# Second attention's query scaling taken to VectorE in a PSUM bank, and its trailing parts from GpSimd to VectorE

## The reference

```
x = x + tanh(g_xattn) * cross_attention(layernorm(x), ctx)          # stage one
y = layernorm(x)                                                     # stage two
q, k, v = y @ Wq.T + bq, y @ Wk.T + bk, y @ Wv.T + bv                # 16 heads of 32
q = (q / norm(q, per head) + query_embedding) * softplus(temperature)
h = softmax(q @ k.T / sqrt(32)) @ v
x = x + tanh(g_ffn) * ((h * gates(h)) @ Wp.T + bp)
```

## Time and profile before

| | |
|---|---|
| median of 3 runs | 5229.36 us |
| the profiled execution's own time | 5233.06 us |
| its span, first to last instruction | 5231.3 us |
| TensorE (PE) matmuls busy | 4810.8 us, 92% |
| VectorE (DVE) busy | 3102.1 us, 59% |
| ScalarE (ACT) busy | 2599.0 us, 50% |
| GpSimd (POOL) busy | 3365.1 us, 64% |
| mean granted TensorE clock | 0.964 |

### The profile page before, as it was taken

The page is one execution under the profiler, slowest core; times in us unless marked ns, Lnnn a source line. Parts: engine busy times, 40 slices in busy tenths (PEclk is TensorE's granted clock), DMA queues, the critical chain, the costliest instruction groups (busy, mean ns, idle before and its releaser), DMA issues.

```text
span 5231.3 us, 67135 instructions
## 1 busy us (share of the span) xinstructions
PE 4810.8 (92%) x21696; PEld 2752.7 (53%) x21696; DVE 3102.1 (59%) x3776; ACT 2599.0 (50%) x4673; POOL 3365.1 (64%) x2667
## 2 busy tenths in 40 slices
PE   4999999999999999998998998998998998989998
PEld 3564555555555555564554554554654544645644
DVE  4555555454546464566766757657657666667663
ACT  2444444343434343546646546546456456456364
POOL 1656656564746565637857757667578487478587
PEclk8999999999999999999999999999999999999998
DMA  7353434343343434332233231322222322322320
GB/s 231 93 143 102 121 108 123 111 119 115 93 129 85 137 85 129 90 100 72 53 97 73 55 108 49 81 81 66 75 79 73 89 60 63 89 75 55 97 49 25
DMA packets 285207, 481.08 MB, mean 92 GB/s; under 512 B 32832, under 2 KB 165440, under 8 KB 275648
## 3 DMA queue, kind: packets, MB, share of 16 engines
q1 hardware_dynamic: 284864, 476.79, 33.6%
HBM read 223.14 MB, written 50.33 MB: 52 GB/s over the span
## 4 chain that ended last, share of the span: by engine, by line
PE 48%; DVE 7%; issue 3%; ACT 2%; POOL 1%; SPq 0%; DMA 0%; ACTq 0%; DVEq 0%; POOLq 0%
PE aux L834 14%; PE acc L937 10%; PE aux L897 9%; PE scores L920 9%; DVE nm L1275 4%; PE aux L949 2%; PE aux L958 1%; DVE rs L1225 1%; PE aux L878 1%; POOL added_f L812 1%; PE aux L854 1%; ACT probs L1122 1%; SPq L729 0%; DMA stack<-ck_lo 0%; ACT xs L1030 0%
## 5 line engine op out<-in xcount | busy, mean ns | idle before, releaser
L1275 DVE TENSOR_REDUCE nm<-aux 128x1 f32<-128x1024 f32 x1536 | 1844.1, 1221 | 1208.8 <-PE aux L897 1205.5
L812 POOL TENSOR_TENSOR added<-added,probs 128x512 f32<-128x512 f32 x1433 | 1805.8, 1297 | 966.2 <-PE acc L937 690.8
L1122 ACT ACTIVATE probs<-scores 128x512 f32<-128x512 f32 x2151 | 1190.0, 597 | 915.4 <-PE scores L920 881.2
L920 PE MATMUL scores<-stack 128*128 128x512 f32 x4096 | 1353.0, 420 | 102.2 <-ACT probs L1122 58.8
L897 PE MATMUL aux<-stack 96*128 96x512 f32 (+1 forms) x3072 | 1023.8, 422 | 132.5 <-DVE nm L1275 96.5
L920 PEld LDWEIGHTS scores<-stack 128*128 128x128 f32 x4096 | 740.7, 191 | 716.7 <-issue 276.4
L937 PE MATMUL acc<-probs,vh 128*32 128x512 f32 (+1 forms) x4302 | 979.8, 623 | 62.2 <-ACT vh L1089 37.9
L897 PEld LDWEIGHTS aux<-stack 96*128 96x128 f32 (+1 forms) x3072 | 529.4, 191 | 618.7 <-DVE nm L1275 319.5
L812 POOL TENSOR_TENSOR added_f<-added_f,probs 128x512 f32<-128x512 f32 x537 | 676.8, 1294 | 57.9 <-PE acc L937 35.9
L834 PE MATMUL aux<-xT_hi,wqk 128*128 128x512 f32 x1536 | 580.6, 407 | 14.8 <-ACT qwork L1061 6.9
L1122 ACT ACTIVATE more<-scores 128x512 f32<-128x512 f32 x537 | 300.3, 598 | 176.7 <-PE scores L920 156.7
(11 more groups left out here) (129 smaller groups left out, 5106.1 us busy)
## 6 DMA issues: line engine op xcount, KB each, us to landing
wqk<-w_split SPq DMA_DIRECT2D x256, 256.0 KB, 3.8
wvo<-w_split SPq DMA_DIRECT2D x64, 1024.0 KB, 6.9
stack<-cq_hi SPq DMA_DIRECT2D x128, 256.0 KB, 5.0
stack<-ck_hi SPq DMA_DIRECT2D x128, 256.0 KB, 5.0
stack<-cq_hi SPq DMA_DIRECT2D x256, 128.0 KB, 2.3
stack<-ck_hi SPq DMA_DIRECT2D x256, 128.0 KB, 2.4
xs<-in_x SPq DMA_DIRECT2D x16, 1024.0 KB, 6.0
stack<-cq_lo SPq DMA_DIRECT2D x64, 256.0 KB, 4.8
```

The lines of the kernel that those rows point to most:

```text
L812: pool.tensor_tensor(onto, onto, exp_buffer(T, e), ALU.add).then_inc(added_ok, 1)
L920: ins = pe.matmul(scores[:, u % SCORES, :], stack[:, g % 2, e * ph.SLOTS + ks, jt * P:(jt + 1) * P], stack[:, g % 2, e * ph.SLOTS + qs, n ...
L1122: act.activation(exp_buffer(T, e), scores[:, (n - 1) % SCORES, :], ACT.Exp, scale=ph.SCALE).then_inc(probs_ok, 1)
L1275: dve.tensor_reduce(nm[:, e * TT + t:e * TT + t + 1], keys, axis=AX.X, op=ALU.max, negate=True).then_inc(emptied["dve"], 1)
```

## The change

`s2` gets a fourth instruction: the product of the corrected reciprocal root and `qb` now stays in the PSUM bank, and VectorE scales and shifts it there with the two per-channel values `tau` and `et`. `s3` on ScalarE is now one instruction, which rounds the bank into `cq_hi`. A new item `s3l` on VectorE takes `cq_lo` from the bank; it takes the place of GpSimd's `s3p` and is what frees the bank of `ss`. `pqa` of the next group waits for `s2` where it waited for `s3p`, and SyncE's `sd` for the bank's release. The planner's times follow (`s2` 2.9, `s3` 0.65, `s3l` 0.7), so that it lists the items of stage two in another order.

```diff
-            before = [("s3p", g - 1, n), ("pqa", g - 1, 1)] + ...
+            before = [("s2", g - 1, n), ("pqa", g - 1, 1)] + ...
...
-            self.add(("s2", g, n), "dve", 2.2, b + 0.3, [("ssa", g, n)])
-            self.add(("s3", g, n), "act", 1.5, b + 0.4, [("s2", g, n), ("sd", g - 1, last_head), ("s3", g, n - 1)])
-            self.add(("s3p", g, n), "pool", 1.3, b + 0.5, [("s3", g, n), ("s3p", g, n - 1)])
+            self.add(("s2", g, n), "dve", 2.9, b + 0.3, [("ssa", g, n)])
+            self.add(("s3", g, n), "act", 0.65, b + 0.4, [("s2", g, n), ("sd", g - 1, last_head), ("s3", g, n - 1)])
+            self.add(("s3l", g, n), "dve", 0.7, b + 0.5, [("s3", g, n), ("s3l", g, n - 1)])
...
-    TAKER = {... "ss": "s2", ...}
+    TAKER = {... "ss": "s3l", ...}
...
-                    elif kind == "s3p":
-                        pool.wait_ge(qs_ok, 2 * q_at["pqa", g, n])
-                        pool.tensor_tensor(cq["lo"][:, q], qy[:, n], cq["hi"][:, q].bitcast(F32), ALU.subtract).then_inc(qlo_ok, 1)
...
                     elif kind == "s3":
-                        wait_emptied(act, ("ss", g, n))
-                        act.activation(qy[:, n], qb[:, n], ACT.Identity, scale=tau[:, g % NG:g % NG + 1], bias=et[:, g % NG:g % NG + 1]).then_inc(qs_ok, 1)
-                        act.wait_ge(qs_ok, 2 * i + 1)
+                        act.wait_ge(qs_ok, s2_at["s2", g, n])
                         if n == 0 and g:
                             wait_stacked(act, g - 1, range(stage((g - 1) // NG).G))
-                        act.activation(cq["hi"][:, n * HALF:(n + 1) * HALF], qy[:, n], ACT.Copy).then_inc(qs_ok, 1)
+                        act.activation(cq["hi"][:, n * HALF:(n + 1) * HALF], aux[:, o.bank["ss", g, n], :], ACT.Copy).then_inc(qhi_ok, 1)
...
                     elif kind == "s2":
-                        dve.tensor_tensor(qb[:, n], qb[:, n], src, ALU.mult).then_inc(emptied["dve"], 1)
+                        link(dve.tensor_tensor(src, src, qb[:, n], ALU.mult))
+                        dve.tensor_scalar(src, src, tau[:, g % NG:g % NG + 1], et[:, g % NG:g % NG + 1], ALU.mult, ALU.add).then_inc(qs_ok, 1)
+                    elif kind == "s3l":
+                        dve.wait_ge(qhi_ok, s3_at["s3", g, n])
+                        dve.tensor_tensor(cq["lo"][:, q], aux[:, o.bank["ss", g, n], :], cq["hi"][:, q].bitcast(F32), ALU.subtract).then_inc(emptied["dve"], 1)
```

More of the change, by code:

```diff
@@ L126 @@
     (1, ("xl", "cx", "cxl", "ln", "la", "lb", "l2", "tr", "tra", "trl", "wv", "wo", "xr")), (2, ("gm",)),
-    (NG, ("wl", "pq", "pk", "pqa", "pka", "pql", "pkl", "ss", "ssa", "s2", "s3", "s3p", "sd", "mx", "mxr", "mt", "ml", "md")),
+    (NG, ("wl", "pq", "pk", "pqa", "pka", "pql", "pkl", "ss", "ssa", "s2", "s3", "s3l", "sd", "mx", "mxr", "mt", "ml", "md")),
     (TT, ("vp", "vpe", "gt", "hs", "hsl", "op", "ope", "xb", "st", "xq")), (HALVES, ("sm", "sma", "ev", "cp")),
@@ L245, in project @@
                 continue
-            before = [("s3p", g - 1, n), ("pqa", g - 1, 1)] + ([("op", TT * j - 1, NG - 1)] if g % NG == 2 else [])
+            before = [("s2", g - 1, n), ("pqa", g - 1, 1)] + ([("op", TT * j - 1, NG - 1)] if g % NG == 2 else [])
             before += [("vp", TT * B - 1, PHASES[0].KC - 1), ("pk", NG * B - 1, 1, PHASES[0].KC - 1)] if g == NG * B else []
@@ L249, in project @@
             self.add(("ss", g, n), "pe", 0.95, b + 0.1, [("pqa", g, n), ("fb", 0)])
-            self.add(("ssa", g, n), "act", 2, b + 0.2, [("ss", g, n), ("s3p", g - 1, n)])
-            self.add(("s2", g, n), "dve", 2.2, b + 0.3, [("ssa", g, n)])
-            self.add(("s3", g, n), "act", 1.5, b + 0.4, [("s2", g, n), ("sd", g - 1, last_head), ("s3", g, n - 1)])
-            self.add(("s3p", g, n), "pool", 1.3, b + 0.5, [("s3", g, n), ("s3p", g, n - 1)])
-        last = "s3p" if ph.ffn else "pql"
+            self.add(("ssa", g, n), "act", 2, b + 0.2, [("ss", g, n), ("s2", g - 1, n)])
+            self.add(("s2", g, n), "dve", 2.9, b + 0.3, [("ssa", g, n)])
+            self.add(("s3", g, n), "act", 0.65, b + 0.4, [("s2", g, n), ("sd", g - 1, last_head), ("s3", g, n - 1)])
+            self.add(("s3l", g, n), "dve", 0.7, b + 0.5, [("s3", g, n), ("s3l", g, n - 1)])
+        last = "s3l" if ph.ffn else "pql"
         before = (g - 1) * STEPS - 1
@@ L403 @@
 class Order:
-    TAKER = {"tr": "trl", "pk": "pkl", "pq": "pql", "ss": "s2", "mt": "ml", "sm": "ev", "vp": "vpe", "op": "ope", "gt": "gm", "mx": "mxr"}
+    TAKER = {"tr": "trl", "pk": "pkl", "pq": "pql", "ss": "s3l", "mt": "ml", "sm": "ev", "vp": "vpe", "op": "ope", "gt": "gm", "mx": "mxr"}
     def __init__(self, items, banks):
@@ L559, in attention @@
         hi_ok = sem("hi_ok")
-        sq_ok, y_ok, qs_ok, qlo_ok = (sem(n) for n in ("sq_ok", "y_ok", "qs_ok", "qlo_ok"))
+        sq_ok, y_ok, qs_ok, qhi_ok = (sem(n) for n in ("sq_ok", "y_ok", "qs_ok", "qhi_ok"))
         scored, probs_ok, weighed = sem("scored"), sem("probs_ok"), sem("weighed")
```

19 lines of the change are left out of this document (8 added, 11 removed).

## The result

The changed kernel takes 5321.77 us in the median of 4 runs (5316.77 to 5325.61), the kernel before 5231.8 in 4 runs beside it: 1.0173 times as long, 95% interval 1.0156 to 1.019. It is 90 us slower where 25 to 30 less were forecast, and lies outside the range of 5158 to 5265. Its profiled span is 5315.0 us.

The account below looks back on a forecast made before the run. TensorE, 92% busy, was taken as the bound. Terms -39 - 31 + 31 + 14 = -25 us against 5233 gave 5208, 5204 for the median, and 5201 us after allowing for overlapping bank waits; range 5158 to 5265.

Parts of the forecast that it names:

- the two holes: TensorE's large idle times in each batch of stage two: 11.9 us at the second norm, 7.62 us at the first gates.
- the 8.32 us: Time of VectorE's 128x4 norm instruction L1225 beside GpSimd's additions, said to agree with the skill's shared port rule.
- Hole A: At a batch's second norm: TensorE's idle time falls from 11.9 to 6.4 us, in 7 batches -39 us.
- Hole B: At a batch's first gates: VectorE meets less of GpSimd's block, TensorE idles 4.4 us less, in 7 batches -31 us.
- The bank: PSUM bank of `ss`, held 8.4 us: TensorE waits 3.9 us a batch for its next product, +31 us in 8 batches.
- The rival of the bank as the bound: The bank's chain takes 11 us, TensorE waits 2.6 us more in five halves a batch: 5305 us, chance 0.17.
- VectorE's work in gaps: VectorE's scaling and difference, 0.7 us each, add 90 us over 64 halves, in gaps for the most part.
- The first norm: At a batch's first norm: TensorE reaches the new batch's first PV early and waits, 2 us in 7 batches, +14 us.
- The clock: TensorE's lower clock after idling: a hole of 6.4 us still brings it, so nothing was given for it.
- the rival: Shorter holes bring the clock back sooner, 3 us in each of 14, the bank costs nothing: 5160 us, chance 0.15.
- The scaling held by GpSimd: Rival: VectorE's scaling is held as L1225 was, 4 us in each of 64 halves: 5400 us, chance 0.03.

Follow-up runs that it names:

- e13: Kernel before, order kept, with the second stage's small norm addition issued by GpSimd in its own queue instead of VectorE: 5193.1 us, ratio 0.9948.
- e5: Changed kernel with the second stage's 64 outputs' remainders issued on GpSimd instead of VectorE, same places in the list: 5300.68 us, ratio 1.0129.
- e9: Kernel before, its order kept, with the scaling alone moved to VectorE, writing SBUF and so freeing the bank: 5252.64 us, ratio 1.005.
- e1: Kernel before's instructions in the changed kernel's order: 5344.01 us, ratio 1.0212 to the kernel before.
- e6: Changed kernel with the last projection of a batch due at step 48 instead of 50: 5279.11 us, ratio 1.0089 to the kernel before.
- e8: Changed kernel with the last projection due at 48 and the second norm after its half's last addition: 5287.88 us, ratio 1.011.
- e7: Kernel before, its second norm of a batch made to wait for its half's last addition, in GpSimd's pause: 5253.43 us, ratio 1.005.
- e12: Kernel before with the last projection due at step 48 instead of 50, nothing else: 5377.93 us, ratio 1.0288.

## Why the prediction was wrong

*What bounds the kernel, and the two holes.* Right. TensorE bounds it, the holes come from small instructions of VectorE beside GpSimd's block, and e13, which takes the norm's one away, gains 32 us on the kernel before. The prediction also says that the 8.32 us agree with the rule it names. They do in kind and not in length: one addition takes some 1.24 us (see the last section).

*Hole A.* Right: L1214 at 3.2 us (4.2 forecast), TensorE idle 4.8 us (6.4), nothing before the transposes. By the holes this gives 7 x 7.1 = 50 us back, where 39 stood in the sum. (1.2 + 2.9 + 4.2 + 2.3 is 10.6, not 10.7, which changes nothing.)

*Hole B.* This step failed. It reads: "From the half's first PV to the gates' product there are 2 scores, 1 pair of maxima and 1 sum more, 2.7 us: VectorE meets 2.7 us less of the block." For the gates that isn't shown: the last of them takes 0.23 us in the median now, but they run behind the hold, from 3015.65 us, when the block has ended at 3006.46. In e5, where nothing holds VectorE ahead of them, one of them meets the block and is held for 8.36 us. And what stands ahead of them on VectorE wasn't looked at. The same shift that carries the gates out of the block carries the outputs' first remainder from 5.65 us into the block, where it took 1.16 us, to 11.7 us in, where it takes 13.56. The prediction read GpSimd's block as something that an instruction leaves by coming later. The idle did not fall by 4.4 us in seven batches (-31 us); a hole of 10.4 us came.

*The bank.* The term was +31 us, by the space between `ss` and the bank's next product. The length of the hold was right (8.2 us, 8.4 forecast). But in the new order it cost TensorE's matmuls no wait for `cq_lo`, in the old one 81.7 us. The price was real, but it was to be read from what the planner did to stay clear of it. The rival of the bank as the bound had the right sign and came within 17 us of the time (5305), by waits that didn't occur: that is luck.

*VectorE's work in gaps.* The scaling took 0.82 us, 0.7 was taken: 8 us over 64 halves. "In gaps for the most part" was too kind: the scaling costs 26 us by itself in the old order (e9).

*The first norm.* Right: TensorE waits 8.1 us for `vh` L1264 and 9.5 for the issue at the batches' first weighings, 17.6 in all, where 14 stood.

*The clock.* "I give nothing for it" missed some 36 us, by the estimate above, on the other side than the rival looked for it.

*The scaling held by GpSimd.* It didn't happen in any of its 64 halves. The rule of the Trainium skill's "SBUF — State Buffer" ("Who interferes with whom"), which names only SBUF operands, agrees with that: L1250 is at 818 ns in median and mean alike. The same rule, applied to every instruction with two inputs in SBUF that the order moves, would have led to L1287.

The loss as measured is one of the order: e1 has it without the new instructions. Of the 90 us the held remainder of the outputs carries up to 43, which e6 gave back by removing that hold, though e6 moves other items too. How the other half divides among many small waits and the clock isn't settled. TensorE's busy time also rose, by 34 us from 2160 us on, about what the lower clock accounts for; in e8, with 11 us of clock, it still rose by 45, and that isn't explained.

## What to carry to other kernels

An engine's busy share says nothing of which instructions another engine holds: before an order is changed, list for each place the instructions of VectorE that GpSimd can hold, and how far into GpSimd's run of additions each of them falls, not only those that are held now. Here the small instruction that is held was best given to the engine that holds it, in its own queue and with the order kept (e13, -32 us), and moving it in time gained nothing (e7, e8). And try to free a shared bank with the first instruction that can write elsewhere: the same work with an early release, in an order of its own, lost 37 us instead of 90.

## What was unexpected of the hardware

An instruction of VectorE that GpSimd holds can be held for a whole run of queued additions, not only the one in progress: 13.56 us for 128x512 in the changed kernel beside 20 additions without a gap, 12.07 in e12, 8.3 for 128x4, each to the end of the run or half a microsecond past it. The Trainium skill, "SBUF — State Buffer", "Who interferes with whom", says that the second to issue blocks until the first is through; these rows go beyond one instruction. Others are held for one addition only: the corrections of the norm in e13 at 1.18 us each, and the kernel before's gates, eight of them one behind the other at 1.08 to 1.33 us beside 14 additions without a gap (2977.19 to 2994.49), the last at 1.19. So a run of GpSimd without a gap doesn't decide between the two by itself, and what does isn't shown.

VectorE's scaling with two per-partition values, bank to bank, takes 818 ns, where the product of the bank with SBUF takes 699 on the same 128x512; from bank to SBUF it takes 809 (e9). And one number of the order, 50 to 48, moved the kernel before by +152 us and the changed kernel by -43.
